# Low words of weights split between GpSimd and VectorE, two root products in split words, counts and masks built earlier

## The reference, cut to what matters

```python
def _rgcn_conv(x, weight, root, bias, src, dst, etype):
    out = x @ root + bias
    for r in range(NUM_REL):
        sel = etype == r
        deg = zeros(n).at[dst].add(sel)
        norm = where(sel, 1.0 / maximum(deg[dst], 1.0), 0.0)
        h_r = x @ weight[r]
        out = out + segment_sum(h_r[src] * norm[:, None], dst, n)
    return out
```

## Time and profile before

| | us |
|---|---|
| timed executions | 883.10, 879.99, 881.56 |
| median | 881.56 |
| the profiled execution | 881.44 |
| its span, first to last instruction | 879.6 |
| TensorE busy | 801.4 |
| VectorE busy | 600.6 |
| GpSimd busy | 517.9 |
| ScalarE busy | 383.9 |

### The profile page before, as it was taken

How to read it: one execution, slowest core, us unless ns; L and a number is a source line. 1 busy time by engine, 2 the same in 40 slices (tenths; PEclk the granted TensorE clock), 3 DMA queues, 4 the chain that set the end, 5 groups by cost and what they waited for, 6 DMA issues and landing times.

```text
span 879.6 us, 10154 instructions
## 1 busy us (share of the span) xinstructions
PE 801.4 (91%) x4034; PEld 631.9 (72%) x4034; DVE 600.6 (68%) x681; ACT 383.9 (44%) x438; POOL 517.9 (59%) x225
## 2 busy tenths in 40 slices
PE   7999999999869999988988779999999998987987
PEld 4569976776546798666655459997997897854674
DVE  8955148999998612989999967535852798254451
ACT  1124366666663433767756424432442342141521
POOL 0346629999996472899999917661873488000000
PEclk9999999999999999999999889999999999988999
DMA  9036515344331552440533238633752653600000
GB/s 366 3 83 240 159 53 162 82 130 149 113 111 65 178 170 94 133 103 1 203 107 109 72 111 284 210 113 119 240 180 72 233 198 108 229 22 1 1 1 36
DMA packets 24262, 110.98 MB, mean 126 GB/s; under 512 B 3604, under 2 KB 5908, under 8 KB 23832
## 3 DMA queue, kind: packets, MB, share of 16 engines
q1 hardware_dynamic: 23096, 104.24, 36.3%
q10 hardware_dynamic: 1120, 6.10, 1.9%
HBM read 100.63 MB, written 0.79 MB: 115 GB/s over the span
## 4 chain that ended last, share of the span: by engine, by line
PE 55%; POOL 30%; DVE 10%; ACT 3%; issue 1%; DMA 0%; DVEq 0%; ACTq 0%
PE ps L946 22%; POOL prod L543 19%; PE ps L894 8%; POOL prod L546 7%; PE ps L931 6%; POOL w_lo L531 4%; DVE prod L1671 4%; PE ps L1323 3%; PE ps L1005 2%; PE ps L1026 2%; PE ps L1382 2%; PE ps L1183 1%; DVE qi_t L1689 1%; PE ps L1308 1%; PE ps L1006 1%
## 5 line engine op out<-in xcount | busy, mean ns | idle before, releaser
L531 POOL TENSOR_TENSOR w_lo<-w_raw,w_hi 128x1536 fp32r<-128x1536 f32 x54 | 201.9, 3750 | 142.7 <-ACT w_hi L597 142.5
L543 POOL TENSOR_TENSOR prod<-prod 128x1024 f32<-128x1024 f32 x94 | 226.8, 2430 | 41.1 <-DVE prod L1671 41.0
L702 ACT ACTIVATE prod<-ps 128x1024 f32<-128x1024 f32 x192 | 188.0, 1024 | 96.0 <-PE ps L1136 73.7
L1671 DVE TENSOR_TENSOR prod<-prod,ps 128x2048 f32<-128x2048 f32 x96 | 218.6, 2278 | 3.2 <-ACT prod L702 2.5
L1136 PE MATMUL ps<-sel_pair,h_and_q 128*128 128x512 f32 x384 | 130.0, 451 | 20.1 <-ACT prod L702 19.8
L597 ACT ACTIVATE w_hi<-w_raw 128x1536 fp32r<-128x1536 f32 x54 | 80.3, 1488 | 136.6 <-PE ps L946 92.1
L894 PE MATMUL ps<-w_raw,h_t 128*128 128x384 f32 x408 | 139.1, 487 | 0.0
L946 PE MATMUL ps<-w_hi,yt_hi 128*128 128x384 f32 x432 | 111.8, 339 | 8.1 <-POOL w_lo L531 8.1
L946 PE MATMUL ps<-w_hi,yt_lo 128*128 128x384 f32 x432 | 110.3, 336 | 0.0
L946 PE MATMUL ps<-w_lo,yt_hi 128*128 128x384 f32 x432 | 110.3, 336 | 0.0
L894 PEld LDWEIGHTS ps<-w_raw,h_t 128*128 128x128 f32 x408 | 77.2, 190 | 45.2 <-issue 0.3
(11 more groups left out here) (188 smaller groups left out, 994.8 us busy)
## 6 DMA issues: line engine op xcount, KB each, us to landing
w_raw<-weights SPq DMA_DIRECT2D x105, 768.0 KB, 4.4
wa_in<-weights SPq DMA_DIRECT2D x6, 768.0 KB, 5.9
w_gat<-weights SPq DMA_DIRECT2D x6, 768.0 KB, 7.9
w_query<-weights SPq DMA_DIRECT2D x3, 768.0 KB, 11.9
h_and_q<-stage_hi SPq DMA_DIRECT2D x24, 96.0 KB, 2.1
h_and_q<-stage_lo SPq DMA_DIRECT2D x24, 96.0 KB, 2.2
a_vec<-gat_vectors ACTq DMA_DIRECT2D x1, 2048.0 KB, 8.1
q_t<-queries ACTq DMA_DIRECT2D x1, 1536.0 KB, 11.1
```

Of the source, the lines that this page charges most:

```text
L531: pool.tensor_tensor(Wl[:, j, :], raw_slab(U, 0, j), Wh[:, j, :], ALU.subtract).then_inc(w_lo_ready, 1)
L543: pool.tensor_tensor(v[:, :, 0:32], v[:, :, 0:32], v[:, :, 32:64], ALU.add).then_inc(folded_once, 1)
L702: act.activation(slot_view(s)[:, :, 32 * u:32 * u + 32], args.rearrange("p b (n l) -> p (b n) l", l=LH), ACT.Sigmoid).then_inc(sigmoid_rea ...
L1671: TT(slot_view(s), slot_view(s), ps[:, 6, o:o + L].unsqueeze(1).broadcast_to([P, NB, L]), ALU.mult).then_inc(products_ready, 1)
```

## The change

Five edits. (1) The low words of slab 2 of every relation are made by VectorE, those of slabs 0 and 1 stay on GpSimd. VectorE makes slab 2 of relation 1 behind relation 1's scaling, that of relation v-1 behind the scaling of relation v = 3 and 4, and that of the last relation behind everything else of the layer. (2) The roots of the fourth and fifth layers are multiplied in split words, like relations: ScalarE makes their high words and the high word of the turned features, VectorE the low words of all three slabs and of the features; they pass through the same single buffer. TensorE takes the root whole ahead of the first aggregate. (3) `counts_of_all` moves to the third layer, behind relation 3. (4) `attention_counts` moves to the fourth layer, behind relation 3, with the transposes it needs. (5) From the third layer on the reciprocal degrees get a place each (`rinv4`) and are computed only in the third layer. In the fifth layer the low words of slab 29.2 stand between the two products on slab 30.0.

```diff
-SPLIT = [UNIT[l] + v + 1 for l in range(LAYERS) for v in range(RELATIONS[l])]
+SPLIT = [UNIT[l] + v for l in range(LAYERS) for v in range(l < 3, RELATIONS[l] + 1)]
+ROOTS = [UNIT[l] for l in range(3, LAYERS)]
...
+LO_BY_VECTOR = [(u, 0, j) for u in SPLIT for j in range(3) if u in ROOTS or j == 2]
+LO_BY_POOL = [(u, 0, j) for u in SPLIT for j in range(2) if u not in ROOTS]
+LO_AT = {key: n + 1 for part in (LO_BY_VECTOR, LO_BY_POOL) for n, key in enumerate(part)}
...
+        rinv4 = sb("rinv4", [P, R4, N], F32, t_off)
...
-            def w_lo(U, js=(0, 1, 2)):
-
-                for j in js:
+            def w_lo(U):
+
+                for j in range(2):
                     pool.wait_ge(w_hi_ready, SPLIT_AT[U, 0, j])
-                    pool.tensor_tensor(Wl[:, j, :], raw_slab(U, 0, j), Wh[:, j, :], ALU.subtract).then_inc(w_lo_ready, 1)
+                    pool.tensor_tensor(Wl[:, j, :], raw_slab(U, 0, j), Wh[:, j, :], ALU.subtract).then_inc(w_lo_by_pool, 1)
...
+            def root_hi(layer, t):
+
+                act.wait_ge(turned[t], layer + 1 if t == 0 else INPUT[layer] + 1)
+                copy(YTh[:, 0, :, t * P:(t + 1) * P], chunk_tile(4 + 2 * t, KC)).then_inc(root_hi_ready[t], 1)
...
                 relations(layer)
                 if layer < LAYERS - 1:
                     relu_out(layer, 0)
-                    keep_turned(layer + 3, layer + 2)
+                    w_hi(UNIT[layer + 1], (0,))
+                    root_hi(layer + 1, 0)
+                    h_hi(layer + 1, 0)
+                    w_hi(UNIT[layer + 1], (1,))
+                    relu_out(layer, 1)
+                    w_hi(UNIT[layer + 1], (2,))
+                    h_hi(layer + 1, 1)
+                    root_hi(layer + 1, 1)
                     w_hi(UNIT[layer + 1] + 1, (0,))
-                    h_hi(layer + 1, 0)
-                    relu_out(layer, 1)
-                    h_hi(layer + 1, 1)
             relu_norm(2, 0, norm_h_ready)
 
...
+            def root_part(layer, t, j):
+
+                if j == 0:
+                    pe.wait_ge(root_lo_ready[t], layer - 2)
+                    root_bias(layer, pair(layer, t))
+                wait_lo(pe, UNIT[layer], j)
+                mm = three_terms(0, j, t, pair(layer, t), False)
+                if t == 1:
+                    mm.then_inc(w_used, 1)
+
+            def three_terms(s, j, t, bank, last):
+
+                for k in (2 * j, 2 * j + 1):
+                    for n, (Y, Wx) in enumerate(((YTh, Wh), (YTh, Wl), (YTl, Wh))):
+                        for h in range(2):
+                            c0 = (k % 2) * F + h * FH
+                            mm = pe.matmul(ps[:, bank + h, 0:FH], Y[:, s, k, t * P:(t + 1) * P], Wx[:, j, c0:c0 + FH],
+                                           start=False, stop=(last and k == KC - 1 and n == 2))
+                return mm
...
             def layer_products(layer, degrees=None):
 
                 e, R = INPUT[layer], RELATIONS[layer]
                 if layer > 2:
-                    root(layer, 0, 0, 4)
-                if layer in (1, 2):
+                    root_part(layer, 0, 0)
+                    turn(1, e)
+                    root_part(layer, 0, 1)
+                    root_part(layer, 0, 2)
+                elif layer > 0:
                     root(layer, 0, 4, KC)
                     turn(1, e)
                 else:
@@ -962,13 +998,18 @@
                     degrees()
                     pe.wait_ge(staged_lo, 2)
                     root(layer, 1, 0, 4)
+                if layer > 2:
+                    for j in range(3):
+                        root_part(layer, 1, j)
                 for t in range(NT):
                     pe.wait_ge(h_lo_ready[t], layer + 1)
-                pe.wait_ge(turn_kept[1], e + 1)
+                if layer < 3:
+                    pe.wait_ge(turn_kept[1], e + 1)
                 if layer == 2:
                     pe.wait_ge(a4_ready, 1)
                 aggregate(layer, 1)
-                root(layer, 1, 4 if degrees is not None else 0, KC)
+                if layer < 3:
+                    root(layer, 1, 4 if degrees is not None else 0, KC)
                 aggregate(layer, 2)
                 for v in range(1, R):
                     for j in range(3):
@@ -977,7 +1018,7 @@
                         mm.then_inc(w_used, 1)
                     if v + 2 <= R:
                         aggregate(layer, v + 2)
-                    if layer == LAYERS - 1 and v == 1:
+                    if layer == 3 and v == 1:
...
+            def root_lo(layer, t):
+
+                dve.wait_ge(root_hi_ready[t], layer - 2)
+                cols = slice(t * P, (t + 1) * P)
+                TT(YTl[:, 0, :, cols], chunk_tile(4 + 2 * t, KC), YTh[:, 0, :, cols], ALU.subtract).then_inc(root_lo_ready[t], 1)
+
+            def w_lo(U, j):
+
+                dve.wait_ge(w_hi_ready, SPLIT_AT[U, 0, j])
+                TT(Wl[:, j, :], raw_slab(U, 0, j), Wh[:, j, :], ALU.subtract).then_inc(w_lo_by_vector, 1)
+
+            def w_lo_beside(layer, v):
+
+                if v != 2:
+                    w_lo(UNIT[layer] + max(v - 1, 1), 2)
 
             def relation(layer, v):
 
                 at_ = BEFORE[layer] + 3 * (v - 1)
                 deg = deg3 if layer < 2 else deg4
-                dve.reciprocal(rinv[:], deg[:, v - 1, :]).then_inc(rinv_ready, 1)
-                dve.wait_ge(rinv_ready, at_ // 3 + 1)
+                inverse = rinv[:] if layer < 2 else rinv4[:, v - 1, :]
+                if layer < 3:
+                    dve.reciprocal(inverse, deg[:, v - 1, :]).then_inc(rinv_ready, 1)
+                    dve.wait_ge(rinv_ready, at_ // 3 + 1)
                 for j in range(4):
                     if j < 3:
                         dve.wait_ge(sums_ready, at_ + (j + 1))
-                        TT(tile3(j), tile3(j), rinv[:].unsqueeze(1).broadcast_to([P, 2, N]),
+                        TT(tile3(j), tile3(j), inverse.unsqueeze(1).broadcast_to([P, 2, N]),
                            ALU.mult).then_inc(sums_scaled, 1)
...
                     relation(i, v)
+                    w_lo_beside(i, v)
+                w_lo(UNIT[i] + RELATIONS[i], 2)
...
             dve.wait_ge(vectors_in, 48)
             for layer in range(2, LAYERS):
                 if layer > 2:
+                    w_lo(UNIT[layer], 0)
+                    root_lo(layer, 0)
                     h_lo(layer, 0)
-                    keep_turned(layer + 2)
+                    w_lo(UNIT[layer], 1)
+                    w_lo(UNIT[layer], 2)
+                    root_lo(layer, 1)
                     h_lo(layer, 1)
                 for v in range(1, RELATIONS[layer] + 1):
-                    if layer == LAYERS - 1 and v == 2:
+                    relation(layer, v)
+                    w_lo_beside(layer, v)
+                    if layer == 2 and v == 3:
                         counts_of_all()
-                    if layer == LAYERS - 1 and v == 4:
+                    if layer == 3 and v == 3:
                         attention_counts()
-                    relation(layer, v)
                     if v % 2 == 0:
                         n = 2 * (layer - 2) + v // 2 - 1
                         dve.wait_ge(wa_in_landed, 16 * n + 16)
                         logit_weights(2 + n // 3, wa_in[:], 2 * (n % 3), 2, n % 3 == 2)
                         dve.wait_ge(wa_product, products[0])
                         dve.nop().then_inc(wa_in_read, 1)
+                if layer == LAYERS - 1:
+                    wait_landed(dve, 30, 0, 0)
+                    logit_weights(0, raw_slab(30, 0, 0), 0, 6, False, (0,))
+                w_lo(UNIT[layer] + RELATIONS[layer], 2)
+                if layer == LAYERS - 1:
+                    logit_weights(0, raw_slab(30, 0, 0), 0, 6, True, (1,))
```

More of the change, by code:

```diff
@@ L230, in build @@
         w_hi_ready = sem("w_hi_ready")
-        w_lo_ready = sem("w_lo_ready")
+        w_lo_by_pool = sem("w_lo_by_pool")
+        w_lo_by_vector = sem("w_lo_by_vector")
         w_used = sem("w_used")
@@ L264, in build @@
         turn_kept = [sem(f"turn_kept{t}") for t in range(NT)]
+        root_hi_ready = [sem(f"root_hi_ready{t}") for t in range(NT)]
+        root_lo_ready = [sem(f"root_lo_ready{t}") for t in range(NT)]
         half_turned = sem("half_turned")
@@ L901, in turn, with root_bias @@
                 ins.then_inc(turned[t], 1)
+            def root_bias(layer, bank):
+                row, slot = ((0, 0), (0, 1), (2, 0), (2, 1), (3, 0))[layer]
+                bias_mm(row, slot, bank)
+            def root_part(layer, t, j):
[14 more added lines that the diff above has]
+                return mm
             def root(layer, t, k0, k1):
@@ L908, in root @@
                     pe.wait_ge(turn_kept[t], e + 1)
-                    row, slot = ((0, 0), (0, 1), (2, 0), (2, 1), (3, 0))[layer]
-                    bias_mm(row, slot, bank)
+                    root_bias(layer, bank)
                 for k in range(k0, k1):
@@ L914, in root @@
```

(18 more changed lines are left out.)

13 lines of the change are left out of this document (5 added, 8 removed).

## The result

The changed kernel took **886.97 us** (median of six, 884.3 to 888.0), the kernel before 879.88 (six, 878.3 to 883.1). The ratio is 1.0075, with a 95% interval from 1.0057 to 1.0094: slower, by 6.6 us by the ratio and 7.1 by the two medians. The forecast was 885.4, in a range from 873.0 to 890.5. The profiled execution has a span of 885.7 us, 6.1 more than before.

A forecast was written before the change was run, and what follows sets the result against it. TensorE, busy 91% of the span, was taken as the bound, with GpSimd and VectorE setting the gate phases' pace. Terms -2.0 + 6.8 + 0.7 - 3.3 + 1.8 = +4.0 on 881.44 gave 885.4 us, range 873 to 890.5.

The forecast's parts named there:

- What GpSimd and VectorE do to each other: Where both read SBUF, their instructions don't overlap: whoever comes second waits to the other's end, then 1.6 or 3.4 us.
- Third layer: In the third layer TensorE waits 1.4, 1.9, 2.1 and 3.2 us for late low words; +6.8 us in all.
- The list of signs: What TensorE's and VectorE's timelines would show: waits before named slabs, each released by VectorE, and logit products at 3.2 us.
- Fourth layer: In the fourth layer: root -3.0, gap between first two aggregates +0.8, end waits of 1.4 and 3.3 us +2.9; together +0.7.
- Fifth layer: In the fifth layer: start -2.2 us, last low word's wait 2.8 instead of 3.9, so -1.1; together -3.3 us.
- clock term: At layer ends, waits of TensorE lower its clock: two drops at 1.8 us instead of one, +1.8 us.
- First and second layers: At the ends of these two layers, slab 2's low word comes 1.7 us sooner, covering the 1.02 wait; -2.0 us together.
- The first rival: In all layers VectorE's low words aren't held up, so end waits, starts and slow matmuls improve: 867 us; chance 0.2.

The follow-up runs named there:

- the fast version: The changed kernel, but VectorE makes the third slab's low word only for each layer's last relation, GpSimd the other relations'; 868.98 us, ratio 0.9863 to the kernel before.

## Why the prediction was right, and where it was off

**The number.** 885.4 for 886.97 looks closer than it was. The forecast added 4.0 to one profiled execution, 881.44, which lies 1.6 above the later median of six, 879.88. The difference forecast was +4.0, the one measured +6.6 to +7.1. So part of the agreement is luck of the base; the sign and the places of the waits are not.

**What GpSimd and VectorE do to each other.** This was the step that everything hung on, and it is shown: the run without the products takes their time back to 1750 ns, the waits to 2.3 us, and the kernel to 868. As the Trainium skill has it ("SBUF — State Buffer", "Who interferes with whom"), a blocked instruction is held to the end of the other. The trace agrees: 3.15 and 5.05 for a product of 1.75.

**Third layer.** The four waits come where the replay (the queues worked through in the rows' durations) put them: 1.22, 1.40, 1.76 and 2.99 for 1.4, 1.9, 2.1 and 3.2. Together 7.4, where 8.1 was taken; with the slow stretch behind them +8.4, for 6.8 + 1.8. The list of signs had each wait released by VectorE; those before 19.1 and 24.1 are released by GpSimd, as the replay itself has it.

**Fourth layer.** 0.92 and 2.96 for 1.4 and 3.3. The start gained 2.1: from the first bias pair to the end of the second aggregate it took 22.56 us before and takes 20.49 now, both read in the fifth layer (673.09 to 695.65, 681.64 to 702.13), with the lost cover in it; the forecast had 2.2 (3.0 - 0.8). With its slow stretch the layer came to +2.8, for 0.7 + 1.8.

**Fifth layer.** 2.82 for 2.8. The layer came to -3.9, where the forecast had -3.3 - 1.8 = -5.1, since by its clock term the slow stretch of before was to go from here. It stayed.

**Clock: the term that was mis-sized.** The forecast took "two drops at 1.8 instead of one: +1.8". Three came, which was priced at +3.6, since the single wait of 2.82 in the fifth layer was also followed by one. Nor does a wait's length decide it: a lone wait of 2.82 before 29.2 had a slow stretch behind it in the changed kernel and none with plain roots (10.15 and 8.60 for the same 48 matmuls), and one of 2.96 to 2.98 before 24.2 had none in the changed kernel with the counts put back, but one in the fast version with the same edit (4.44 and 6.00 for 24). What decides isn't settled; no run was made on it alone. The price of 1.8 was a little high, too: 0.3 of it is the restart, which comes without a drop as well. With 1.5 to 1.6 each, three stretches for one of before are +3.0, for the +1.8 of the forecast: nearly all of the 1.3 by which the three layers missed it.

**First and second layers: too small.** "Gain 1.0 each." The first layer's last 24 matmuls begin 1.63 sooner (at 111.13 instead of 112.76), but 0.31 of that was there when the layer began (49.89 and 50.20). From its first bias pair to them it takes 61.24 instead of 62.56 us, and the second layer, from its first aggregate to its last 24 matmuls, 50.85 instead of 52.14: 1.3 each. The wait of 1.02 is only the part of the gap that the trace books as a wait; the restart behind it (4.43 for 24 matmuls that take 4.18) went as well. The start of the third layer is a weaker measure, since it moves with the gates: with this part in, eleven traces have it from 513.2 to 517.3; in the two without it is at 518.5 and 519.4.

Sum of the terms so corrected, for the three layers: 8.4 + 2.8 - 3.9 = +7.3 where the forecast had 6.8 + 0.7 - 3.3 + 1.8 = +6.0; 2.6 gained ahead of them for 2.0; and 1.4 behind them that no term covers. The first rival's time of 867 didn't come with the low words where the change puts them; with fewer of them handed over, the other edits as they are, 869.0 did.

## What to carry to other kernels

Before work is handed from one engine to another, ask whether the two can read at the same time; if not, the work still costs the first engine its turn, and what counts is the place in the second's queue. Hand over only the piece that the bound engine waits for last, here one low word in each layer: with the other parts alike, five moved low words made the kernel 1.4% faster than before, eighteen 0.75% slower. Then measure parts together, since one (the counts' move) can be worth nothing until another (the split roots) makes its place critical.

## What the runs showed of the hardware

I took the hold to be for instructions with two tiles in SBUF only. Copies, casts and operations with a constant, which read a single tile, are held too (below, the COPY and the TENSOR_SCALAR; the other three rows read two). In the fast version with the counts back, VectorE's timeline beside low words of GpSimd (two from 686.92, six in a row from 700.38):

```profile
687.55 3.87 DVE L1861 TENSOR_TENSOR count<-count,a_i 128x512 f32<-128x512 f32 x1
691.46 3.62 DVE L1862 COPY count<-count 128x512 f32<-128x512 f32 x1
...
713.14 3.60 DVE L1874 TENSOR_SCALAR logit_rows<-ident 128x256 fp32r<-128x256 f32 x1
716.66 4.53 DVE L1875 TENSOR_TENSOR sel_src<-ident 128x1024 fp32r<-128x1024 f32 x1
721.11 3.47 DVE L1877 TENSOR_TENSOR sel_dst<-ident 128x8 fp32r<-128x8 f32 x1
```

Before the change, in the same places, the copy took 0.43, the step on logit_rows 0.29, that on sel_src 1.22, and the one on sel_dst, 8 elements wide, 0.16. The cast took 0.22 before and 2.94 in the changed kernel:

```profile
642.16 2.94 DVE L1873 CAST ident_b<-ident 128x128 bf16<-128x128 f32 x1
```

So a tiny instruction costs some 3.5 us if its turn comes behind a long one (3.47 for the 8 elements); and where both engines have work, they take turns, one instruction each (713.14, 716.66, 721.11 each wait for one low word). The Trainium skill says that copies, casts and operations with a constant can contend with GpSimd, in the modes that use both ports ("SBUF — State Buffer", "Who interferes with whom"), and these rows agree. Reductions, reciprocals (1.75) and scalings out of PSUM were not longer in any of these traces.
